# A gated mixture of experts after a conditional layer: hidden units numbered by chunk, the shared expert moved three tiles ahead, and the opening reordered

## The chip, the cores and the metric

The kernel runs on one core of one Trainium2 chip. The engines used are TensorE (PE), VectorE (DVE), ScalarE (ACT), GpSimd (POOL), and SyncE, whose queue (SPq) issues most of the DMAs. The metric is the device time of one execution in microseconds (us), lower is better.

## The reference, cut to what matters

```python
x = x + gelu(x @ W.T + fc_bias + z + cond)      # z: low-rank product with fside, per sample
# 32 samples of 128 tokens, 128 features; then a mixture of 4 experts and a shared one:
gate_logits = gate_in @ gate_w + gate_b         # gate_in: means over three token segments
gate_logits = gate_logits * (1.0 + scale) + shift
w_be = top-2 of softmax(gate_logits), renormalized
for e in range(4):                              # experts 1 and 2 skip one token segment
    h = gelu_tanh(x @ ew1[e] + eb1[e])          # 128 -> 512
    out += w_be[:, e] * mask[e] * (h @ ew2[e] + eb2[e])   # 512 -> 128
shared = gelu_tanh(x @ sw1 + sb1) @ sw2 + sb2
return x + out + shared
```

## The kernel before, in words

Features lie on the partitions, tokens on the free axis. The 32 samples make 8 tiles of 4 samples (512 tokens). The first four tiles pass the conditional layer at the start: transposes of x and fside, `matrices` (a 128x128 matrix per sample), `matrix` on DVE (adds W), `layer0`, `gelu0` on ACT, `residual` on DVE. Then each tile's x is split into a high and a low fp32r part (`x1_high` on ACT, `x1_low` on DVE), as are all expert weights (`weight_high` on ACT, `weight_low` on DVE), since each product is made as three fp32r matmuls (L449, L450, L451). Tiles 4 to 7 pass the conditional layer later, a step at a time between the experts (`late_tile`).

The middle layer has 512 hidden units in 4 chunks of 128. The work from there is a list `STEPS` of 40 units (t, s): tile t, s = 0 for the shared expert and 1 to 4 for the experts. Unit k goes through four stages:

- `up(k)` on PE: 4 chunks of 3 matmuls, each chunk into a PSUM bank of its own out of the ring `RING` (5 banks).
- `gelu(k)` on ACT: reads each bank, writes `h`. For a shared unit a second pass over the same bank writes `hs_hi`, the rounded high part; since `hs_hi` has two buffers, all of `gelu` for a shared unit waits until `down(k-2)` is done.
- `split(k)` on DVE: for an expert `hs_hi` (L695) and `hs_lo` (L700), both scaled by the sample's gate weight; for a shared unit `hs_lo` alone (L689).
- `down(k)` on PE: 12 matmuls that sum into `psY[t % 2]`, one bank per tile in work. When a tile's last unit is done, DVE adds it to x (`out_sum`), PE transposes, ACT copies out.

PE's order is written out by hand: `up(k + 2)`, then `down(k)`. A shared unit (t + 2, 0) stands behind the last expert of tile t; its `down` waits until `out_sum(t)` has read the sum bank of tile t. Experts 2 and 3 skip one segment and have 344 columns, the others 512. The gate of tiles 0 to 3 (`segment_sums`, `time_gate`, `gate_in`, `modulation`, `gate_logits`, `gate_weights` on DVE, two small products on PE, `gate_tanh` on ACT) runs at the start, and must be done before the first expert's `split`. POOL adds the output biases to x (L308) once they are known (`bias2_ok`).

The wait in `up` on the ring, and the one in `gelu`:

```python
                    else:
                        pe.wait_ge(h_ok, n - UP + 1)
...
                if s == 0 and k >= 2:
                    act.wait_ge(down_ok, k - 1)
```

Of the kernel before, what the change touches and what calls it, by code (L numbers as in the profile page):

```python
# [12 lines left out]
def build(nc, x, fside, cond, W, fc_bias, gate_w, gate_b, time_w, time_b,  # L13
# [40 lines left out]
    with ExitStack() as ctx:  # L54
# [18 lines left out]
        eb2_raw = sb("eb2_raw", [E, D])  # L73
        b1_col = sb("b1_col", [128, NS, CH])
# [80 lines left out]
            sem("tanh_g_ok"), sem("w_ok"), sem("bias2_ok"), sem("x1b_ok"))  # L155
        up_ps, h_ok, hi_ok, lo_ok, down_ok = sem("up_ps"), sem("h_ok"), sem("hi_ok"), sem("lo_ok"), sem("down_ok")
# [73 lines left out]
        def _(sp):  # L230
# [12 lines left out]
            def load_weight(n):  # L243
# [33 lines left out]
        def _(pool):  # L277
# [35 lines left out]
        def _(act):  # L313
# [49 lines left out]
            def gelu(k):  # L363
# [7 lines left out]
                for c in range(CH):  # L371
# [3 lines left out]
                    if s == 0:  # L375
# [71 lines left out]
        def _(pe):  # L447
# [5 lines left out]
            def keep_busy(n):  # L453
# [451 lines left out]
```

## Time and profile before

| | us |
|---|---|
| median of 3 runs | 276.78 (276.58 to 278.21) |
| the profiled execution | 276.94 |
| its span, first to last instruction | 274.8 |
| PE busy | 244.4 (89%) |
| DVE busy | 198.8 (72%) |
| ACT busy | 156.2 (57%) |
| POOL busy | 22.2 (8%) |

The span is 2.1 us shorter than the profiled execution's own time. A matmul's end is modelled in the profile and overlaps the next one, so the distance between two starts is what a matmul costs PE.

### The profile page before, as it was taken

To read this page: it belongs to the slowest core of one execution; us is meant where nothing else is said; L and a number is where in the kernel's file an instruction comes from. 1 tells how busy PE (TensorE), PEld (TensorE's weight loads), DVE (VectorE), ACT (ScalarE), POOL (GpSimd) and SP (SyncE) were. 2 spreads that over 40 slices of the span, in tenths; PEclk is the share of its full clock that TensorE was granted. 3 is DMA by queue.
4 is the path that set the end of the run, shared out by engine and by line. 5 is a ranking of instruction groups with operands and counts; after the bars stand their busy time and mean duration, and the time that the engine had idled before them with its cause. 6 is when DMAs were issued, how large, how long until landed. Compare 5 with 4: busy or idle time off the path is not lost.

```text
span 274.8 us, 3451 instructions
## 1 busy us (share of the span) xinstructions
PE 244.4 (89%) x1217; PEld 203.2 (74%) x1217; DVE 198.8 (72%) x441; ACT 156.2 (57%) x286; POOL 22.2 (8%) x39
## 2 busy tenths in 40 slices
PE   8964969799979997999989997999979989999963
PEld 7763748678768875888768885887768959898852
DVE  0266799999369565797399795797499959779661
ACT  4375799630894439760894439751835194544400
POOL 5000000940000000000000060000000600000000
PEclk9995598999999999999999999999999999999987
DMA  6995000000001000010001000010001000100101
GB/s 129 235 284 96 1 1 0 0 2 0 0 2 38 0 0 4 6 32 2 1 0 38 2 0 0 6 36 0 0 0 41 0 0 0 43 0 0 38 0 38
DMA packets 15811, 7.40 MB, mean 27 GB/s; under 512 B 6175, under 2 KB 14515, under 8 KB 15795
## 3 DMA queue, kind: packets, MB, share of 16 engines
q1 hardware_dynamic: 14781, 6.98, 10.6%
q10 hardware_dynamic: 854, 0.18, 0.3%
q8 instruction: 9, 0.15, 0.2%
q0 software_dynamic: 160, 0.02, 0.1%
q14 instruction: 7, 0.06, 0.1%
HBM read 5.09 MB, written 2.10 MB: 26 GB/s over the span
## 4 chain that ended last, share of the span: by engine, by line
PE 61%; ACT 16%; DVE 14%; issue 4%; DMA 2%; SPq 2%; DVEq 0%; ACTq 0%
PE ps L449 19%; PE ps L451 17%; PE ps L450 17%; ACT h L373 5%; ACT hs_hi L376 4%; DVE hs_lo L700 4%; DVE hs_hi L695 3%; PE ps L496 2%; DMA x_tok<-in_x 2%; DVE W_lo L679 2%; ACT L373 2%; ACT L354 2%; PE ps L508 2%; DVE hs_lo L689 2%; ACT W_raw L359 2%
## 5 line engine op out<-in xcount | busy, mean ns | idle before, releaser
L373 ACT ACTIVATE h<-ps,b_col 128x512 f32<-128x512 f32 (+1 forms) x160 | 94.1, 649 | 60.5 <-PE ps L451 38.4
L700 DVE SCALAR_TENSOR_TENSOR hs_lo<-h,w_be,hs_hi 128x512 fp32r<-128x512 f32 (+1 forms) x128 | 78.4, 673 | 0.0
L449 PE MATMUL ps<-x_hi,W_hi 128*128 128x512 f32 (+1 forms) x160 | 65.1, 407 | 14.2 <-ACT h L373 5.5
L449 PE MATMUL ps<-hs_hi,W_hi 128*128 128x512 f32 (+1 forms) x160 | 59.9, 375 | 6.3 <-DVE hs_lo L700 4.9
L695 DVE TENSOR_SCALAR hs_hi<-h,w_be 128x512 fp32r<-128x512 f32 (+1 forms) x128 | 50.3, 455 | 13.7 <-ACT h L373 6.9
L451 PE MATMUL ps<-x_lo,W_hi 128*128 128x512 f32 (+1 forms) x160 | 60.0, 375 | 0.0
L450 PE MATMUL ps<-x_hi,W_lo 128*128 128x512 f32 (+1 forms) x160 | 59.8, 374 | 0.0
L451 PE MATMUL ps<-hs_lo,W_hi 128*128 128x512 f32 (+1 forms) x160 | 59.0, 369 | 0.0
L450 PE MATMUL ps<-hs_hi,W_lo 128*128 128x512 f32 (+1 forms) x160 | 59.0, 369 | 0.0
L449 PEld LDWEIGHTS ps<-x_hi,W_hi 128*128 128x128 f32 x160 | 30.8, 192 | 27.9 <-ACT hs_hi L376 10.8
L449 PEld LDWEIGHTS ps<-hs_hi,W_hi 128*128 128x128 f32 x160 | 30.6, 191 | 11.6 <-DVE hs_lo L700 2.8
L689 DVE TENSOR_TENSOR hs_lo<-h,hs_hi 128x1024 fp32r<-128x1024 f32 x16 | 18.9, 1221 | 24.8 <-ACT hs_hi L376 24.8
L451 PEld LDWEIGHTS ps<-x_lo,W_hi 128*128 128x128 f32 x160 | 30.9, 193 | 4.5
L308 POOL TENSOR_TENSOR x<-x,bias 128x168 f32<-128x168 f32 (+1 forms) x24 | 18.2, 789 | 196.6 <-DVE bias L812 196.6
L451 PEld LDWEIGHTS ps<-hs_lo,W_hi 128*128 128x128 f32 x160 | 30.6, 191 | 4.3
L450 PEld LDWEIGHTS ps<-hs_hi,W_lo 128*128 128x128 f32 x160 | 30.7, 192 | 4.2
L450 PEld LDWEIGHTS ps<-x_hi,W_lo 128*128 128x128 f32 x160 | 31.1, 194 | 3.1
L376 ACT ACTIVATE hs_hi<-ps,b_col 128x512 fp32r<-128x512 f32 x32 | 22.8, 711 | 0.0
L391 ACT ACTIVATE x_tok<-ps 128x512 f32<-128x512 f32 x8 | 4.8, 598 | 28.6 <-PE ps L562 28.6
L327 ACT ACTIVATE x<-ps 128x512 f32<-128x512 f32 x8 | 4.8, 597 | 17.9 <-PE ps L466 17.9
L712 DVE TENSOR_TENSOR outT<-ps,x 128x168 f32<-128x168 f32 (+1 forms) x24 | 6.5, 327 | 5.3 <-PE ps L451 5.2
L654 DVE SCALAR_TENSOR_TENSOR h<-ps,WT 128x512 f32<-128x512 f32 x4 | 2.8, 689 | 9.3 <-PE ps L496 9.3
(102 smaller groups left out, 173.4 us busy)
## 6 DMA issues: line engine op xcount, KB each, us to landing
W_raw<-in_L_cond_ew SPq DMA_DIRECT2D x8, 256.0 KB, 4.9
out<-x_tok SPq DMA_DIRECT2D x8, 256.0 KB, 2.3
x_tok<-in_x SPq DMA_DIRECT2D x6, 168.0 KB
x_tok<-in_x SPq DMA_DIRECT2D x3, 176.0 KB
W_raw<-in_L_cond_sw SPq DMA_DIRECT2D x2, 256.0 KB, 5.0
x_tok<-in_x SPq DMA_DIRECT2D x3, 84.0 KB
F_raw<-in_fside_Bx1x1024x SPq DMA_DIRECT2D x3, 64.0 KB, 5.3
x_tok<-in_x SPq DMA_DIRECT2D x2, 88.0 KB
```

The source lines that it names most:

```text
L308: nc.gpsimd.tensor_tensor(xb[:, :, at:at + n], xb[:, :, at:at + n], bias2[:, i, t * NB:(t + 1) * NB].unsqueeze(2).to_broadcast([128, NB, n ...
L354: nc.scalar.activation(table_probe[:, 1:2], table_probe[:, 0:1], ACT.Gelu)
L359: ins = nc.scalar.activation(g0_late[:, b * L:(b + 1) * L], psLate[:, b * L:(b + 1) * L], ACT.Gelu, bias=bias0[:, t * NB + b:t * NB + b + 1])
L373: ins = nc.scalar.activation(span(h[:, k % 3, c, :], s), up_bank(k, c), ACT.Gelu_apprx_tanh, bias=b1_col[:, s, c:c + 1])
L376: ins = nc.scalar.activation(hs_hi[:, k % 2, c, :], up_bank(k, c), ACT.Gelu_apprx_tanh, bias=b1_col[:, s, c:c + 1])
L449: nc.tensor.matmul(dst, w_hi, m_hi, start=start, stop=False)
L450: nc.tensor.matmul(dst, w_lo, m_hi, start=False, stop=False)
L451: return nc.tensor.matmul(dst, w_hi, m_lo, start=False, stop=stop)
L689: nc.vector.tensor_tensor(hs_lo[:, k % 2, c:c + 2, :], h[:, k % 3, c:c + 2, :], f32(hs_hi[:, k % 2, c:c + 2, :]), ALU.subtract).then_inc(l ...
L695: nc.vector.tensor_scalar(hs_hi[:, k % 2, :, c], h[:, k % 3, :, c], w_be[:, t * NB + b, s - 1:s], None, ALU.mult).then_inc(hi_ok, 1)
L700: nc.vector.scalar_tensor_tensor(hs_lo[:, k % 2, :, c], h[:, k % 3, :, c], w_be[:, t * NB + b, s - 1:s], f32(hs_hi[:, k % 2, :, c]), ALU.m ...
L712: nc.vector.tensor_tensor(dst_v[:, :, dst:dst + n], sum_v[:, :, at:at + n], x1_v[:, :, at:at + n], ALU.add).then_inc(outT_ok, 1)
```

## The change

- The hidden units are numbered by chunk: unit c*128+p instead of 4p+c. The columns of the first weights that a chunk takes are then contiguous in SBUF instead of 16 bytes apart; the second weights come as four rows of 512 bytes for each partition instead of one of 2048. The biases `b1` come as 20 rows and are turned by a PE transpose and a DVE copy.
- `STEPS` begins with three shared units, and the shared unit behind tile t's last expert is that of tile t + 3. Bank 3 goes from the ring (now 4 banks) to `psY` (now 3).
- For a shared unit ACT writes the high part of two chunks only; DVE writes the other two with one cast from `h` (128x1024).
- In the opening DVE's `segment_sums`, `time_gate` and `output_rows` stand later; PE makes `up(0)` ahead of the gate's first product and `up(1)` ahead of its second, with six small products on ones in front; ACT rounds one more weight ahead of `gelu(0)`; `output_biases(0)` stands at unit 5.
- POOL waits, for tile t, until the split two units ahead of the tile's first expert is done.

```diff
-    STEPS = [(0, 0), (1, 0)]
+    AHEAD = 3
+    STEPS = [(t, 0) for t in range(AHEAD)]
     for t in range(NT):
         STEPS += [(t, s) for s in range(1, NS)]
-        if t + 2 < NT:
-            STEPS.append((t + 2, 0))
+        if t + AHEAD < NT:
+            STEPS.append((t + AHEAD, 0))
...
-    RING = [0, 1, 4, 2, 3]
+    RING = [0, 1, 4, 2]
...
-        psY = [ps[:, 5, :], ps[:, 6, :]]
+        psY = [ps[:, 5, :], ps[:, 6, :], ps[:, 3, :]]
...
-                return W1_raw[:, e, :].rearrange("p (m c) -> p c m", c=CH), W1_hi[:, e, :, :], W1_lo[:, e, :, :]
+                return W1_raw[:, e, :].rearrange("p (c m) -> p c m", c=CH), W1_hi[:, e, :, :], W1_lo[:, e, :, :]
...
-                    sp.dma_start(W2_raw[:, e, :], src.rearrange("(p c) d -> p (c d)", c=CH)).then_inc(w_in[n], 16)
+                    sp.dma_start(W2_raw[:, e, :].rearrange("p (c d) -> p c d", c=CH),
+                                 src.rearrange("(c p) d -> p c d", c=CH)).then_inc(w_in[n], 16)
...
+                pool.wait_ge(lo_ok, parts_until(first_step(t) - 2))
...
-                    if s == 0:
+                    if s == 0 and c < CH // 2:
                         ins = nc.scalar.activation(hs_hi[:, k % 2, c, :], up_bank(k, c), ACT.Gelu_apprx_tanh,
...
-                if s == 0 and t >= 2:
-                    pe.wait_ge(outT_ok, NSEG * (t - 1))
+                if s == 0 and t >= AHEAD:
+                    pe.wait_ge(outT_ok, NSEG * (t - AHEAD + 1))
...
                 if s == 0:
+                    nc.vector.tensor_copy(hs_hi[:, k % 2, CH // 2:, :], h[:, k % 3, CH // 2:, :]).then_inc(shared_hi_ok, 1)
                     for c in range(0, CH, 2):
+                        if c == CH // 2:
+                            dve.wait_ge(shared_hi_ok, t + 1)
```

DVE's order in the opening, before, from the residual of tile 1 on (h<-ps,WT is `matrix`, segsum `segment_sums`, the rows from silu2 to gw `time_gate`):

```order
L661 TENSOR_TENSOR x1<-x1,h 128x512
L666 TENSOR_TENSOR x1_lo<-x1,x1_hi 128x512
L673 TENSOR_REDUCE segsum<-x1 128x8 x3
L717 SCALAR_TENSOR_TENSOR silu2<-tanh_c,condT 128x32
L720 TENSOR_SCALAR tw<-time_w_raw 128x8
L722 TENSOR_TENSOR mod_terms<-silu2,tw 128x256
L726 TENSOR_SCALAR gw_full<-gate_raw 128x4
L727 SCALAR_TENSOR_TENSOR gw<-gate_raw,gw_full 128x4
L729 SCALAR_TENSOR_TENSOR gw<-gate_raw,gw_full 128x4
L730 SCALAR_TENSOR_TENSOR gw<-gate_raw,gw 128x4
L736 COPY eb2T<-ps 128x4 x3
```

The `matrix` of tile 3 stands behind all of these. The same place on DVE now:

```order
L674 TENSOR_TENSOR x1<-x1,h 128x512
L679 TENSOR_TENSOR x1_lo<-x1,x1_hi 128x512
L667 SCALAR_TENSOR_TENSOR h<-ps,WT 128x512
L674 TENSOR_TENSOR x1<-x1,h 128x512
L679 TENSOR_TENSOR x1_lo<-x1,x1_hi 128x512
L753 COPY eb2T<-ps 128x4 x3
L755 COPY b1_col<-ps 128x20
L757 MEMSET eb2T 128x1
L758 MEMSET eb2T 128x1
L692 TENSOR_TENSOR W1_lo<-W1_raw,W1_hi 128x512
L686 TENSOR_REDUCE segsum<-x1 128x8 x3
```

The `matrix` of tile 3 now comes right behind the low part of tile 0, and the low part of the first weight ahead of all gate work.

ACT's order at a shared unit that is followed by a late tile's gelu, before (it repeats for every late tile):

```order
L373 ACTIVATE h<-ps,b1_col 128x512 x5
L376 ACTIVATE hs_hi<-ps,b1_col 128x512
L373 ACTIVATE h<-ps,b1_col 128x512
L376 ACTIVATE hs_hi<-ps,b1_col 128x512
L373 ACTIVATE h<-ps,b1_col 128x512
L376 ACTIVATE hs_hi<-ps,b1_col 128x512
L373 ACTIVATE h<-ps,b1_col 128x512
L376 ACTIVATE hs_hi<-ps,b1_col 128x512
L354 ACT_TABLE_LOAD
L354 ACTIVATE table_probe<-table_probe 128x1
L359 ACTIVATE W2_raw<-ps,bias0 128x128 x4
L373 ACT_TABLE_LOAD
```

And now:

```order
L381 ACTIVATE h<-ps,b1_col 128x512 x5
L384 ACTIVATE hs_hi<-ps,b1_col 128x512
L381 ACTIVATE h<-ps,b1_col 128x512
L384 ACTIVATE hs_hi<-ps,b1_col 128x512
L381 ACTIVATE h<-ps,b1_col 128x512 x2
L362 ACT_TABLE_LOAD
L362 ACTIVATE table_probe<-table_probe 128x1
L367 ACTIVATE W2_raw<-ps,bias0 128x128 x4
L381 ACT_TABLE_LOAD
```

Two of the eight passes over the unit's banks are gone from ACT.

## Rows read from the trace of the kernel before

**Rows 1.** The page, part 2: granted TensorE clock in tenths, 40 slices of 6.87 us

```profile
PEclk9995598999999999999999999999999999999987
```

**Rows 2.** View of the waits, whole run: us in total, times, longest

```profile
PE ps L449 <- ACT h L373: 5.5, 4, 1.5
...
PE ps L449 <- DVE W_lo L679: 4.9, 2, 2.7
...
PE ps L449 <- ACT hs_hi L376: 3.8, 14, 0.7
```

**Rows 3.** Timeline of the opening: start, length, engine, line; idle before and releaser

```profile
18.73 1.33 DVE L673 TENSOR_REDUCE segsum<-x 128x8 f32<-128x336 f32 x3
...
21.74 0.69 DVE L654 SCALAR_TENSOR_TENSOR h<-ps,WT 128x512 f32<-128x512 f32 x1
...
22.54 2.05 PE L508 MATMUL ps<-x,h 128*128 128x128 f32 x8 [3.99 <-issue]
...
24.62 1.14 ACT L348 ACTIVATE h<-ps,bias 128x128 f32<-128x128 f32 x4 [3.39 <-PE ps L508]
...
28.12 0.80 PE L449 MATMUL ps<-x_hi,W_hi 128*128 128x512 f32 x1 [2.68 <-DVE W_lo L679]
...
29.85 1.28 ACT L373 ACT_TABLE_LOAD   x1 [1.54 <-PE ps L451]
...
33.77 0.23 DVE L766 TENSOR_TENSOR logit<-ps,gate_mul 128x64 f32<-128x64 f32 x1 [1.69 <-PE ps L576]
...
37.08 1.68 DVE L679 TENSOR_TENSOR W_lo<-W_raw,W_hi 128x512 fp32r<-128x512 f32 x2
```

**Rows 4.** Stretches of 1 us: busy by engine, granted clock, DMA share, GB/s

```profile
15.00:16.00 1.00, 1.00 (x11) 0.96 (x10) 0.81 (x2) 0.99 (x2) 0.00 (x0) 1.00 1.06 397
...
20.00:21.00 1.00, 0.00 (x0) 0.00 (x0) 0.91 (x6) 1.00 (x2) 0.00 (x0) 0.50 1.05 154
```

**Rows 5.** Timeline of the first units (35 to 70 us)

```profile
48.62 9.69 POOL L308 TENSOR_TENSOR x<-x,bias 128x168 f32<-128x168 f32 x12 [43.45 <-DVE bias L812]
...
51.84 3.60 DVE L700 SCALAR_TENSOR_TENSOR hs_lo<-h,w_be,hs_hi 128x512 fp32r<-128x512 f32 x4
...
55.59 0.47 PE L449 MATMUL ps<-hs_hi,W_hi 128*128 128x512 f32 x1 [2.37 <-DVE hs_lo L700]
```

**Rows 6.** Timeline around one shared unit in the middle (70 to 90 us)

```profile
69.81 0.69 ACT L373 ACTIVATE h<-ps,b_col 128x512 f32<-128x512 f32 x1 [7.28 <-PE ps L451]
...
74.24 0.39 PE L449 MATMUL ps<-hs_hi,W_hi 128*128 128x512 f32 x1
...
74.56 1.28 ACT L354 ACT_TABLE_LOAD   x1
...
76.99 0.32 PE L449 MATMUL ps<-x_hi,W_hi 128*128 128x344 f32 x1
...
78.40 4.17 ACT L373 ACTIVATE h<-ps,b_col 128x512 f32<-128x512 f32 x8
79.14 0.43 PE L449 MATMUL ps<-x_hi,W_hi 128*128 128x344 f32 x1 [1.51 <-ACT h L373]
...
80.85 1.67 DVE L695 TENSOR_SCALAR hs_hi<-h,w_be 128x512 fp32r<-128x512 f32 x4 [2.31 <-ACT h L373]
80.88 0.40 PE L449 MATMUL ps<-hs_hi,W_hi 128*128 128x512 f32 x1
...
85.09 1.32 DVE L695 TENSOR_SCALAR hs_hi<-h,w_be 128x344 fp32r<-128x344 f32 x4
```

**Rows 7.** View by tile, `W_hi` and `W_lo`: length in ns, min/median/max

```profile
L323 ACT ACTIVATE W_hi<-W_raw x10: 641/942/1280, 20.1 to 49.1; 128x512 fp32r<-128x512 f32 x10
L679 DVE TENSOR_TENSOR W_lo<-W_raw,W_hi x10: 679/1005/1253, 27.0 to 61.6; 128x512 fp32r<-128x512 f32 x10
```

**Rows 8.** Timeline at the last gate group (190 to 204 us)

```profile
192.46 0.50 PE L449 MATMUL ps<-x_hi,W_hi 128*128 128x512 f32 x1 [0.71 <-ACT hs_hi L376]
...
202.03 0.50 PE L449 MATMUL ps<-hs_hi,W_hi 128*128 128x512 f32 x1 [1.40 <-DVE outT L712]
```

More of the change, by code:

```diff
@@ L415, in _ @@
             weight_high(WEIGHTS[2])
-            act.wait_ge(b1_in, 32)
+            weight_high(WEIGHTS[3])
+            act.wait_ge(b1_ok, 1)
             gelu(0)
             gate_tanh(0)
-            weight_high(WEIGHTS[3])
             gelu(1)
@@ L451, in product3, with keep_busy @@
                 return nc.tensor.matmul(dst, w_hi, m_lo, start=False, stop=stop)
-            def keep_busy(n):
+            def keep_busy(n, dst=psIdle):
                 for _ in range(n):
-                    nc.tensor.matmul(psIdle, ones[:, :], ones[:, :], start=True, stop=True)
+                    nc.tensor.matmul(dst, ones[:, :], ones[:, :], start=True, stop=True)
             def xT(t):
@@ L539, in down @@
                     pe.wait_ge(w_lo_ok, made(2 * s + 1))
-                if s == 0 and t >= 2:
-                    pe.wait_ge(outT_ok, NSEG * (t - 1))
+                if s == 0 and t >= AHEAD:
+                    pe.wait_ge(outT_ok, NSEG * (t - AHEAD + 1))
+                elif s == 0 and t == 2:
+                    pe.wait_ge(g0_ok, NA)
                 elif s == 0 and t == 1:
@@ L546, in down @@
                 for c in range(CH):
[L547 removed]
+                    last = product3(span(psY[t % AHEAD], s), W2_hi[:, s, c, :], W2_lo[:, s, c, :],
                                     span(hs_hi[:, k % 2, c, :], s), span(hs_lo[:, k % 2, c, :], s),
@@ L601, in _ @@
                     nc.tensor.transpose(psEb2T, eb2_raw[:, :], ident[0:E, 0:E]).then_inc(eb2T_ps, 1)
+                    pe.wait_ge(b1_in, 16 * 2)
+                    nc.tensor.transpose(psB1, b1_rows[:, :], ident[0:NS * CH, 0:NS * CH]).then_inc(b1_ps, 1)
+            keep_busy(6, ps[:, 6, 0:128])
+            up(0)
             pe.wait_ge(eb2T_read, NSEG)
+            pe.wait_ge(b1_ok, 1)
             pe.wait_ge(mod_terms_ok, 1)
             nc.tensor.matmul(psMod, ones[:, :], mod_terms[:, :, :], start=True, stop=True).then_inc(mod_ps, 1)
-            up(0)
+            up(1)
             logits(0)
-            up(1)
             for k in range(K):
@@ L709, in out_sum @@
                 dst_v, sum_v, x1_v = (ap.rearrange("p (b l) -> p b l", l=L)
-                                      for ap in (outT[:, t % 2, :], psY[t % 2], x1[:, t, :]))
+                                      for ap in (outT[:, t % 2, :], psY[t % AHEAD], x1[:, t, :]))
                 for at, dst, n in SEGS:
@@ L827, in _ @@
                     x1_low(t - 1)
-                if t == 1:
+                if t == 2:
+                    output_rows()
+                    weight_low(WEIGHTS[0])
                     segment_sums(0, 2)
-                    time_gate()
-                    output_rows()
-            weight_low(WEIGHTS[0])
             segment_sums(2, 4)
+            time_gate()
             gate_in(0)
+            x1_low(NA - 1)
             dve.wait_ge(bias_in, 16 * 3)
             modulation()
-            x1_low(NA - 1)
-            gate_logits(0)
             weight_low(WEIGHTS[1])
             weight_low(WEIGHTS[2])
+            gate_logits(0)
             split(0)
@@ L844, in _ @@
             split(1)
-            weight_low(WEIGHTS[4])
-            output_biases(0)
-            weight_low(WEIGHTS[5])
+            for n in WEIGHTS[4:6]:
+                weight_low(n)
             for k in range(2, K):
```

15 lines of the change are left out of this document (10 added, 5 removed).

## The prediction, made before the changed kernel ran

> **What bounds the kernel now.** I read the page's clock line, then the waits of PE, then the timeline at each place where PE waits. PE sets the end: it is 89% busy, and its work is the same in both kernels but for a few small products, so only its waiting and its clock can change. A chunk of three 512-column matmuls costs 0.69 us: from 74.24 to 76.99 twelve of them run without a gap, 0.23 us each [rows 6]. PE's lost time lies in four places.
> (a) The opening. DVE works on the segment sums at 18.73 and gets to tile 3's `matrix` only at 21.74; `layer0` of tile 3 starts at 22.54, after 3.99 us idle, and by 20 us the granted clock is at 0.50, its lower level [rows 3, 4]. `up(0)` starts at 28.12, held by the first weight's low part, and its matmuls run at that level [rows 1, 3].
> (b) The first units. PE waits 2.2 us for a low weight (4.9 in two waits, 2.7 of it at 28.12) and 2.37 for `hs_lo` of the first expert, which ends late since POOL's twelve adds run beside it: that `hs_lo` takes 3.60 us, while a whole split of 512 columns elsewhere takes 4.24, from 80.85 to 85.09 [rows 2, 3, 5, 6].
> (c) Each shared unit in the middle. ACT may start it only when `down(k-2)` is done, then makes eight passes at 0.58 us (69.81 to 74.56), and behind them, at four of the six, a late tile's gelu with two table loads. PE waits on its banks (14 waits of 3.8 us in all) and then 1.5 us for the next gelu [rows 2, 6].
> (d) Near 202 us: `down` of a shared unit waits 1.40 us for `out_sum`, which stands behind the gate's work on DVE [rows 8].
>
> **The opening, step by step.** Until 18.7 nothing moves by more than 0.2 us (one 20-row transpose more; the bias rows are issued earlier than before). Tile 3's `matrix` takes DVE's place of 18.73 and ends at 19.4, `layer0` follows until 20.4 (full clock) or 21.3 (half). DVE then has residual and low part of tile 1 and 2 (0.6 us each), the small copies, and the first `weight_low`: 22.4. ACT's first `weight_high` is of the contiguous kind, 0.64 us instead of 1.12, and `weight_low` 0.68 instead of 1.06: the two ends of Rows 7, since the second weights were contiguous before and the first were not [rows 7]. The six small products fill PE until 21.7 to 23.5. So `up(0)` starts at 22.5 to 23.5 instead of 28.12, at full clock for 2.76 us: done by 25.2 to 26.3.
> ACT: `gelu0` of tile 3 (1.14 us) ends at 22.2, then high parts; it waits for DVE's residual of tile 3 (24.35, behind 1.33 us of segment sums), rounds two more weights (26.3), loads the table (1.28) and makes six passes: chunks are free at 28.8, 29.9, 30.5 and 31.1. Before, the load began at 29.85 [rows 3]: 3.6 us later. `up(1)` follows these chunks and ends at 32.0, or at 33.5 if the clock has fallen during PE's waits; the gate's product follows, and DVE's `gate_logits` starts at 32.3 to 33.8, where it was at 33.77 [rows 3]. Here almost all of the opening's gain is given back: the gate chain is as late as before. It takes 3.3 us as before (33.77 until the two weights at 37.08 [rows 3]). Then `split(0)`: two subtractions as before and a cast, 2.3 + 0.7 us.
> The cast has one source and 1024 columns. Below: the same rate as the one-source L695, which takes 1.67 us for four of 512 and 1.32 us for four of 344, so 0.52 ns per column, 0.42 + 512 x 0.00052 = 0.68 us. Above: the two-source rate, twice the 0.68 of a contiguous `weight_low`, 1.36 us [rows 6, 7]. I take 0.7, the nearer kind of instruction. Of what no row shows, the Trainium skill, "VectorE: DVE Perf Modes", section "Mode 2×_2P — use both read ports for one tensor", says that a one-source copy within SBUF makes two results a cycle even in fp32 and a two-source one can't; by it the cast would be near the lower bound, by the other bound DVE has 0.7 us more in each of eight units.
> So `split(0)` ends at 38.6 to 40.1, `down(0)` (2.75 us) at 41.3 to 42.8. Now a new wait: the third unit, (2,0), is a shared one, so `gelu(2)` starts only at the end of `down(0)`, D. Its chunks are free at D + 1.2, 2.3, 2.9, 3.5; `up(3)` ends at D + 4.2 (1.4 us lost), `down(1)` at D + 7.0, `up(4)` at D + 8.9, `down(2)` at D + 11.7, `up(5)` and the late transposes at D + 14.1. DVE ends `split(2)` at D + 7.4 and the first expert's at D + 12.9 (4.3 us, without POOL beside it), so PE no longer waits there. Then `down(3)`, the first expert's, begins at 55.4 to 56.9, where it was at 55.59 [rows 5], but with one more shared unit done, 24 x 0.23 = 5.5 us of PE work. A last 0.4 us comes from the order of the late tile's work. **Gain of the opening:** 5.5 + 0.4 + (55.59 - 55.4) = 6.1, or 4.6 at the late end; with 1.2 us more off if the clock falls a second time between `up(1)` and `up(2)`, 3.4. I take 4.9.
>
> **A shared unit in the middle.** With four banks a chunk of the next `up` waits for the same chunk's gelu, not for the chunk before. In Rows 6's case chunks are free at 71.1, 72.2, 72.8, 73.4 (two with two passes, two with one); the fourth chunk runs 73.7 to 74.4, and `down` starts at 74.4 instead of 74.24: the ring costs what the two passes save. Behind it ACT's last pass ends at 73.4 instead of 74.56, so table loads, late gelu and the next gelu are 1.15 us early: that gelu starts at 77.25 instead of 78.40 and its four chunks, 0.58 us apart, are free at 77.9, 78.5, 79.1, 79.7. The following `up` (344 columns, 0.48 us a chunk) ends at 80.2 instead of 80.88 [rows 6]: gain 0.68. Four such units: **2.7**. DVE's cast is hidden: DVE was idle 2.31 us ahead of 80.85 [rows 6]; were it not, it would cost 0.7 a unit.
> There are now five shared units in the middle instead of six, and the one that goes is without a late gelu; PE lost 0.71 us in one wait there [rows 8], 0.2 in each of the two that follow it and about 0.5 in slowed starts: **1.6**. The one in the opening is counted above.
>
> **The third sum bank.** `down` of a shared unit waits for a sum of three tiles back, long read. The 1.40 us goes, with 0.2 of slowed start [rows 8]; next late is `hs_lo` of the following expert, 1.8 us away from PE's new arrival minus the cast. **1.6.**
>
> **The rest at nothing.** The second weights come in short rows. While long rows land the DMAs move 397 GB/s, while x's 512-byte rows land 154 [rows 4]: 256 KB take 1.7 us instead of 0.66, five loads some 5 us more. The last would land near 24 us and is rounded after 48; cover gone only if the first, wanted at 22.9, came 8 us late. POOL's adds now run in threes beside DVE's idle time ahead of a shared unit; if not, 2.4 us of POOL stretch DVE by 0.9 us x 3/12 each. The tail (PE waits for the last `hs_lo`, and the clock falls behind it [rows 1]) is unchanged.
>
> **Sum.** 4.9 + 2.7 + 1.6 + 1.6 = 10.8 off the profiled 276.94 gives 266.1, off the median 266.0.
>
> **Rivals.**
> 1. The ring takes the middle's gain. If a short ring costs a chunk (0.69) at each of five shared units instead of 0.15, 2.7 us go, and another 0.8 where no late gelu follows: 266.0 + 3.5 = 269.5. For it: PE already waits on the banks 14 times. Against: the start times above. Chance 0.17.
> 2. The clock stays low through the opening. PE's work from 25 to 40 us is now in pieces with waits of 1 to 2.5 us, and in this trace the clock fell in a wait of 3.99 us and again after the one of 2.2 (the seventh slice) [rows 1, 3]. At half clock a chunk costs 1.28 instead of 0.69: `up(1)`, `up(2)`, `down(0)` and `up(3)` 16 x 0.59 = 9.4, of which waits cover nearly half; 4.9 us are lost: 270.9. Chance 0.10. The Trainium skill, "TensorE: Matmul & The Clock Gate", section "What's actually happening", has the same thing as a rule: the throttled state is the default and activity releases it; by it the six filling products are too few for these waits.
> 3. Slower: four banks bind at every unit. `up(k+2)` can't start until `gelu(k+1)` has freed its first bank; that is hidden as long as ACT is less than one `down` (1.9 to 2.75 us) behind. If ACT fell behind by more, each of 37 units would lose a chunk's gelu less the cover, 0.35 us or more: 13 us, so 279. It decides from ACT's lag of 2.75 us on. Against: ACT is 57% busy, and away from shared units PE has no wait on it [rows 2]. Chance 0.04.
> 4. The opening gives nothing: DVE, busy without a pause, gets the casts and a third split ahead of the first expert and is late by as much as PE gains. 266.0 + 4.9 = 270.9, and with rival 1 274.4, no change. 0.05 for the first, 0.04 for the second.
>
> **Chances.** The forecast (264 to 268.5) 0.60; rivals 0.17, 0.10, 0.04, 0.09. The range must take in rivals 1 and 2 and, below, an opening at full clock with DVE's last waits gone (2 us): 263.0 to 271.5. A difference under 1% is about what a measurement of this kernel can't tell. Faster by over 1% (below 274.0) 0.90, within 1% 0.06, slower 0.04.
>
> **What would show it.** In the new trace: `up(0)` starts near 23 at the clock's upper level; `gate_logits` near 33; the first expert's `down` near 56, without a wait; PE's wait behind each late gelu about 0.8 instead of 1.5; no wait of PE on `outT`; the cast 0.7 us. Wrong if PE waits on `h` at ordinary units, if the cast takes 1.2 us or more, or if the clock line shows more fives than before.

## The result, and the profile after

| | before | after |
|---|---|---|
| median, us (range, runs) | 277.24 (276.58 to 278.21, 4) | 268.47 (265.95 to 271.4, 4) |
| the profiled execution | 276.94 | 265.95 |
| its span | 274.8 | 264.2 |
| mean granted clock in it | 0.958 | 0.996 |
| PE busy | 244.4 (89%) | 239.3 (91%) |
| DVE busy | 198.8 (72%) | 197.3 (75%) |
| ACT busy | 156.2 (57%) | 145.4 (55%) |
| POOL busy | 22.2 (8%) | 15.2 (6%) |

The ratio after to before is 0.959, with a 95% interval of 0.954 to 0.965; it and the ratios of the experiments leave out executions over 1.5% above the fastest of their kernel, and the two medians alone give 0.968. The median stands between two levels at which the changed kernel comes out, 265.95 and 266.08 us at a mean granted clock of 0.996 and 0.990, and 270.86 and 271.4 at 0.975 and 0.973; the profiled execution is one of the upper clock.

The page's clock line, that answers to [rows 1]:

```profile
PEclk9999999999999999999999999999999999999998
```

No slice is below nine tenths but the last: the two fives and the eight of the opening are gone. The view of the waits of PE (in all, times, longest), that answers to [rows 2]:

```profile
PE ps L457 <- ACT hs_hi L384: 8.5, 12, 2.6
PE ps L457 <- DVE hs_lo L717: 2.5, 1, 2.5
PE ps L457 <- ACT h L381: 2.2, 4, 0.6
PE ps L457 <- DVE outT L729: 1.9, 2, 1.4
...
PE ps L457 <- DVE hs_lo L706: 0.4, 1, 0.4
PE ps L457 <- DVE W_lo L692: 0.3, 1, 0.3
```

The wait for low weights went from 4.9 to 0.3 us and that for the late gelu (`h`) from 5.5 to 2.2. The wait on the banks (`hs_hi`) grew from 3.8 to 8.5, 2.6 of it once in the opening, and `outT` is still there. The opening's timeline (start, length, engine, line; idle before and releaser), answering to [rows 3, 5]:

```profile
19.07 1.13 PE L516 MATMUL ps<-x,h 128*128 128x128 f32 x8 [0.90 <-issue]
...
21.80 0.50 PE L457 MATMUL ps<-x_hi,W_hi 128*128 128x512 f32 x1 [0.26 <-DVE W_lo L692]
...
28.02 0.47 PE L457 MATMUL ps<-x_hi,W_hi 128*128 128x512 f32 x1 [1.12 <-DVE x_lo L679]
...
31.63 0.23 DVE L785 TENSOR_TENSOR logit<-ps,gate_mul 128x64 f32<-128x64 f32 x1 [1.04 <-PE ps L584]
...
34.22 0.47 PE L457 MATMUL ps<-x_hi,W_hi 128*128 128x512 f32 x1 [2.62 <-ACT hs_hi L384]
...
38.04 0.47 PE L457 MATMUL ps<-hs_hi,W_hi 128*128 128x512 f32 x1 [0.40 <-DVE hs_lo L706]
...
42.57 0.47 PE L457 MATMUL ps<-x_hi,W_hi 128*128 128x512 f32 x1 [1.50 <-ACT hs_hi L384]
```

`layer0` of tile 3 waits 0.90 us instead of 3.99, and `up(0)`, `up(1)`, `up(2)`, `down(0)` and `up(3)` start at 21.80, 28.02, 34.22, 38.04 and 42.57. The middle shared unit of [rows 6]:

```profile
69.78 0.69 ACT L381 ACTIVATE h<-ps,b_col 128x512 f32<-128x512 f32 x1 [7.28 <-DVE hs_lo L717]
...
71.11 0.50 PE L457 MATMUL ps<-x_hi,W_hi 128*128 128x512 f32 x1 [0.52 <-ACT hs_hi L384]
...
73.40 0.69 DVE L702 CAST hs_hi<-h 128x1024 fp32r<-128x1024 f32 x1 [3.63 <-ACT h L381]
...
74.47 0.40 PE L457 MATMUL ps<-hs_hi,W_hi 128*128 128x512 f32 x1
...
77.23 4.18 ACT L381 ACTIVATE h<-ps,b_col 128x512 f32<-128x512 f32 x8
...
77.97 0.43 PE L457 MATMUL ps<-x_hi,W_hi 128*128 128x344 f32 x1 [0.58 <-ACT h L381]
```

The late gelu's successor starts at 77.23, 1.17 us earlier than in [rows 6], and PE waits 0.58 us for it instead of 1.51. The place of [rows 8]:

```profile
200.43 0.50 PE L457 MATMUL ps<-hs_hi,W_hi 128*128 128x512 f32 x1 [1.40 <-DVE outT L729]
```

The length of this wait is unchanged: the one that the third sum bank was thought to remove is still 1.40 us.

### The profile page after: what moved, and what is told of

The parts are those of the page before. It is cut to its first block, busy times and chain, and to the rows that moved or that the text cites. A ratio compares the mean times of both kernels' runs of the same rounds, so it can differ in the third digit from the quotient of the medians.

```text
span 264.2 us, 3479 instructions
## 1 busy us (share of the span) xinstructions
PE 239.3 (91%) x1230; PEld 200.3 (76%) x1230; DVE 197.3 (75%) x450; ACT 145.4 (55%) x270; POOL 15.2 (6%) x39
## 3 DMA queue, kind: packets, MB, share of 16 engines
q1 hardware_dynamic: 16069, 6.98, 10.8%
## 4 chain that ended last, share of the span: by engine, by line
PE 69%; ACT 14%; DVE 11%; issue 4%; DVEq 0%; POOL 0%; ACTq 0%; POOLq 0%
PE ps L457 20%; PE ps L459 19%; PE ps L458 19%; ACT h L381 5%; DVE hs_lo L717 4%; PE ps L504 3%; ACT hs_hi L384 3%; DVE hs_hi L712 3%; ACT L381 2%; PE ps L474 2%; PE ps L463 2%; PE ps L488 1%; ACT L362 1%; PE ps L570 1%; ACT W_raw L367 1%
## 5 line engine op out<-in xcount | busy, mean ns | idle before, releaser
L381 ACT ACTIVATE h<-ps,b_col 128x512 f32<-128x512 f32 (+1 forms) x160 | 92.7, 641 | 63.8 <-PE ps L459 38.0
L717 DVE SCALAR_TENSOR_TENSOR hs_lo<-h,w_be,hs_hi 128x512 fp32r<-128x512 f32 (+1 forms) x128 | 76.2, 657 | 0.0
L457 PE MATMUL ps<-x_hi,W_hi 128*128 128x512 f32 (+1 forms) x160 | 63.3, 395 | 12.5 <-ACT hs_hi L384 8.5
L459 PE MATMUL ps<-x_lo,W_hi 128*128 128x512 f32 (+1 forms) x160 | 58.5, 366 | 0.0
L458 PE MATMUL ps<-x_hi,W_lo 128*128 128x512 f32 (+1 forms) x160 | 58.5, 365 | 0.0
L712 DVE TENSOR_SCALAR hs_hi<-h,w_be 128x512 fp32r<-128x512 f32 (+1 forms) x128 | 48.5, 441 | 12.2 <-PE ps L459 7.9
L458 PEld LDWEIGHTS ps<-x_hi,W_lo 128*128 128x128 f32 x160 | 30.2, 189 | 3.1
L316 POOL TENSOR_TENSOR x<-x,bias 128x168 f32<-128x168 f32 (+1 forms) x24 | 11.1, 491 | 215.9 <-DVE hs_lo L717 134.1
L702 DVE CAST hs_hi<-h 128x1024 fp32r<-128x1024 f32 x8 | 5.5, 692 | 17.4 <-ACT h L381 17.4
L384 ACT ACTIVATE hs_hi<-ps,b_col 128x512 fp32r<-128x512 f32 x16 | 11.0, 689 | 0.0
```

Source lines behind the costliest of these rows:

```text
L316: nc.gpsimd.tensor_tensor(xb[:, :, at:at + n], xb[:, :, at:at + n], bias2[:, i, t * NB:(t + 1) * NB].unsqueeze(2).to_broadcast([128, NB, n ...
L381: ins = nc.scalar.activation(span(h[:, k % 3, c, :], s), up_bank(k, c), ACT.Gelu_apprx_tanh, bias=b1_col[:, s, c:c + 1])
L384: ins = nc.scalar.activation(hs_hi[:, k % 2, c, :], up_bank(k, c), ACT.Gelu_apprx_tanh, bias=b1_col[:, s, c:c + 1])
L457: nc.tensor.matmul(dst, w_hi, m_hi, start=start, stop=False)
L458: nc.tensor.matmul(dst, w_lo, m_hi, start=False, stop=False)
L459: return nc.tensor.matmul(dst, w_hi, m_lo, start=False, stop=stop)
```

## The experiments

All start from the changed kernel; the medians of before on the same chips were 277.1, 277.5 and 277.3 us. The table has medians in us with range and number of executions, the ratio to before with its 95% interval, and the mean granted clock of each execution. Differences of medians below hold the clock too; where two kernels stand at different levels, the text also compares executions at like clocks, or the starts of the same `down` in the two profiles.

| run | median (range, runs) | ratio [95%] | clocks |
|---|---|---|---|
| act_writes_all | 275.6 (273.1 to 279.5, 10) | 0.995 [0.990, 1.000] | .963 to .996 |
| old_dve_opening | 273.0 (271.9 to 273.5, 4) | 0.984 [0.980, 0.988] | .962 .966 .962 .962 |
| old_numbers | 272.7 (268.9 to 273.2, 4) | 0.976 [0.966, 0.985] | .972 .962 .977 .966 |
| two_ahead | 264.5 (263.2 to 265.3, 4) | 0.957 [0.951, 0.962] | .989 .985 .990 .983 |
| two_ahead_ring4 | 269.2 (268.8 to 270.0, 4) | 0.974 [0.970, 0.979] | .978 .978 .976 .990 |
| sum_before_gate | 269.2 (265.7 to 269.7, 4) | 0.966 [0.958, 0.975] | .990 .968 .968 .968 |
| fill_waits | 266.0 (265.6 to 267.3, 5) | 0.958 [0.954, 0.962] | .994 .994 .994 .994 .996 |
| no_six | 268.3 (265.4 to 270.8, 4) | 0.960 [0.953, 0.967] | .975 .982 .971 .990 |
| pool_free | 269.3 (265.8 to 271.8, 4) | 0.962 [0.955, 0.970] | .989 .990 .968 .967 |
| dve_casts_all | 256.4 (255.3 to 258.2, 4) | 0.928 [0.922, 0.935] | .975 .980 .980 .980 |
| best_two_ahead | 254.8 (254.7 to 258.2, 4) | 0.924 [0.916, 0.931] | .995 .982 .999 .989 |
| best_sum_first | 252.5 (252.2 to 252.6, 4) | 0.912 [0.907, 0.917] | .996 to .999 |

**The cast undone: act_writes_all.** ACT writes the high part of all four chunks again, nothing else is changed.

```diff
-                    if s == 0 and c < CH // 2:
+                    if s == 0:
...
-                    nc.vector.tensor_copy(hs_hi[:, k % 2, CH // 2:, :], h[:, k % 3, CH // 2:, :]).then_inc(shared_hi_ok, 1)
...
-                        if c == CH // 2:
-                            dve.wait_ge(shared_hi_ok, t + 1)
```

> The changed kernel with ACT writing the high part of all four chunks of a shared unit, and no cast on DVE. Theory A (ACT's passes are on the path at every shared unit): each of five middle units ends 0.85 to 1.15 us later, the opening 1 to 2: 271 to 273 us. Rival (the passes are hidden, the change's gain comes from the opening alone): 266 to 267.

Measured: 7 us slower than the change, more than expected, and the same between the two executions at a clock of .996 (273.1 against 265.95); what is left can't be told from before. The first line of the view of PE's waits:

```profile
PE ps L457 <- ACT hs_hi L384: 11.2, 26, 2.6
```

The banks now hold PE 26 times instead of 12, and the starts of ACT at the shared units lie 31.4 us apart (72.22, 103.59, 134.94) instead of 30.2. With a ring of four banks the two passes that the cast saves are worth 1.15 us for each middle unit.

**The opening on DVE undone: old_dve_opening.** `segment_sums(0, 2)`, `time_gate` and `output_rows` stand behind the residual of tile 1 again.

```diff
+                dve.wait_ge(b1_ps, 1)
...
+                if t == 1:
+                    segment_sums(0, 2)
+                    time_gate()
+                    output_rows()
                 if t == 2:
-                    output_rows()
                     weight_low(WEIGHTS[0])
-                    segment_sums(0, 2)
             segment_sums(2, 4)
-            time_gate()
```

> The changed kernel with DVE's segment sums, time gate and small rows back ahead of tile 3's matrix. Theory A (tile 3 comes 3 us later, the clock falls in that wait, and gelu(0) starts 3 us later): 3 to 5 us more than the changed kernel. Rival (DVE does the same work in either order and is the bound of the opening): within 1 us.

Measured: 4.6 us slower at the medians, clock included; in the profiles the first expert's `down` starts at 59.62 instead of 55.55. PE again waits for tile 3's `matrix`, `up(0)` starts at 25.82 instead of 21.80, and the clock falls in every execution (.962 to .966). One line of the view of PE's waits, and the clock line of this kernel:

```profile
PE ps L516 <- issue: 3.9, 1, 3.9
```

```profile
PEclk9986979899999999999999999999979999999979
```

**The numbering undone: old_numbers.** Weights, their loads and the biases are laid out as before (unit 4p+c).

```diff
-                return W1_raw[:, e, :].rearrange("p (c m) -> p c m", c=CH), W1_hi[:, e, :, :], W1_lo[:, e, :, :]
+                return W1_raw[:, e, :].rearrange("p (m c) -> p c m", c=CH), W1_hi[:, e, :, :], W1_lo[:, e, :, :]
...
-                    sp.dma_start(W2_raw[:, e, :].rearrange("p (c d) -> p c d", c=CH),
-                                 src.rearrange("(c p) d -> p c d", c=CH)).then_inc(w_in[n], 16)
+                    sp.dma_start(W2_raw[:, e, :], src.rearrange("(p c) d -> p (c d)", c=CH)).then_inc(w_in[n], 16)
```

> The changed kernel with the hidden units numbered as before (columns 16 bytes apart, long rows of the second weights, biases loaded in place). Theory A (three first weights stand on ACT ahead of the first gelu, 0.5 us each, and one on DVE ahead of up(0), 0.4): the opening is 1.5 to 2.5 us later, and the clock falls more often: 2 to 5 us more than the changed kernel's median of 268.5. Rival (hidden): within 1 us.

Measured: 4.2 us slower at the medians, 2.9 between the fastest executions, which is what was expected. `up(0)` starts at 22.60 and the first gelu at 28.38 instead of 26.61, behind weights that ACT rounds at the slow rate of [rows 7]; the clock is lower too (.962 to .977).

**Two tiles ahead: two_ahead and two_ahead_ring4.** The first has `AHEAD` 2, the ring of five (and the wait for its fifth bank's first use) and two sum banks, as before, with all else of the change; the second is the same without the line of `RING`.

```diff
-    AHEAD = 3
+    AHEAD = 2
...
-    RING = [0, 1, 4, 2]
+    RING = [0, 1, 4, 2, 3]
...
-        psY = [ps[:, 5, :], ps[:, 6, :], ps[:, 3, :]]
+        psY = [ps[:, 5, :], ps[:, 6, :]]
```

> The changed kernel with the shared expert two tiles ahead again, so with five ring banks and two sum banks; everything else of the change stays. Theory A (the gain is the opening's order, plus one middle shared unit fewer): the opening loses nothing, one shared unit more stands in the middle and costs 1.6 us; 267 to 268 us against 266 in executions at the upper clock. Rival (three ahead is what hides the gate at the start): the first expert's split comes too late for PE, 3 us or more are lost, 270 or above.

> As two_ahead, but with four ring banks, bank 3 unused: the price of the fifth bank alone. Theory A (a chunk waits for ACT's pace either way, 0.15 us per middle shared unit): within 0.8 us of two_ahead. Rival (the ring binds at shared units, 0.7 us at each of six): 4 us more than two_ahead.

Measured: 264.5 and 269.2. The first is faster than either of its expectations. The fifth bank is worth 4.7 us at the medians and 4.3 between the executions at a clock of .990 (264.54 and 268.85). Of the change's parts the step to three tiles ahead, bought with that bank, costs 1.5 us against the change's executions at the upper clock (266.0), and 4.0 at the median, where the change's lower level counts too. The step alone, with four banks in both kernels, gains: 268.85 against 266.08 at .990, 2.8 us. PE's largest waits, of two_ahead and then of two_ahead_ring4:

```profile
PE ps L457 <- ACT hs_hi L384: 4.9, 11, 1.8
PE ps L457 <- ACT h L381: 3.0, 4, 0.8
PE ps L457 <- DVE hs_lo L719: 2.5, 1, 2.5
PE ps L457 <- DVE outT L731: 1.8, 2, 1.4
```

```profile
PE ps L457 <- ACT hs_hi L384: 8.6, 13, 2.6
...
PE ps L457 <- ACT h L381: 2.2, 4, 0.6
PE ps L457 <- DVE outT L729: 1.9, 2, 1.4
```

With five banks the wait on the ring is 3.7 us less and that for `h` 0.8 more; the shared units follow each other at 29.6 us (63.17, 92.80, 122.43) and not at 30.2 (66.17, 96.38, 126.61). In the profiles 3.0 of the two kernels' difference is there by the first expert's `down` (48.95 and 51.97), and 3.8 come after it. These are the timelines of `up(1)`, with five banks and with four:

```profile
28.02 0.50 PE L457 MATMUL ps<-x_hi,W_hi 128*128 128x512 f32 x1 [0.34 <-ACT hs_hi L384]
```

```profile
28.26 0.77 PE L457 MATMUL ps<-x_hi,W_hi 128*128 128x512 f32 x1 [1.12 <-DVE x_lo L679]
```

At 28.02 the first is in its second chunk, having made one from 26.64 on in the free bank; the second only begins, and at half clock (0.77 us for the matmul), so a part of the 3.0 is clock. And `outT` is waited for with two banks and two ahead just as with three and three.

**The late gate behind the sum: sum_before_gate.** `gate_logits` of a late group moves from ahead of `out_sum` to behind it.

```diff
                 if s == NS - 1:
                     out_sum(t)
+                g = late_gate(k, 5)
+                if g is not None:
+                    gate_logits(g)
                 split(k)
...
-                g = late_gate(k, 4)
-                if g is not None:
-                    gate_logits(g)
```

> The changed kernel with gate_logits of the late groups behind out_sum on DVE instead of ahead of it. Theory A (a shared unit's down still waits for the sum of the tile just finished, since t + 3 and t have the same of three banks): PE's waits for outT, 1.4 and 0.5 us, go: 1.5 to 2 us less than the changed kernel. Rival (PE then waits for hs_lo of the next expert, as gate_logits delays that all the same): under 0.5 us.

Measured: 265.67 in one execution, 268.7 to 269.7 at a clock of .968 in three. Of the change's executions two took 265.95 and 266.08, and two took 270.9 and 271.4. The time of the profiled execution, 0.3 us less than the change's, hides what the edit does; the two profiles show it. First the last `down` of the changed kernel, then of this one:

```profile
256.29 0.50 PE L457 MATMUL ps<-hs_hi,W_hi 128*128 128x512 f32 x1 [2.54 <-DVE hs_lo L717]
```

```profile
203.62 0.51 PE L457 MATMUL ps<-hs_hi,W_hi 128*128 128x512 f32 x1 [0.36 <-DVE hs_lo L717]
...
254.43 0.50 PE L457 MATMUL ps<-hs_hi,W_hi 128*128 128x512 f32 x1 [2.54 <-DVE hs_lo L717]
```

Both waits on the sum bank are gone. `down(7,0)` starts at 197.96 instead of 200.43, the `down` behind it waits 0.36 us for `hs_lo`, and the last `down` starts 1.9 us earlier: 0.8 of that comes from the wait at 141 us and 1.0 from that at 200 us. Then the clock takes 1.6 us of it back. The stretch, columns as in [rows 4]:

```profile
256.00:257.00 1.00, 1.00 (x4) 0.71 (x3) 0.00 (x0) 0.00 (x0) 0.00 (x0) 0.50 0.00 0
```

The last `down` takes 4.60 us here and 3.04 in the changed kernel's profile. So theory A holds, and not the rival.

**The clock: fill_waits and no_six.** The first puts small products on ones, whose sums nobody reads, into PE's waits: 6 behind `up(0)`, 2 ahead of `up(1)`, 11 behind the gate's product, 10 ahead of the last `down`. The second leaves out the six that the change has ahead of `up(0)`.

```diff
             up(0)
+            keep_busy(6, ps[:, 6, 0:128])
...
+            keep_busy(2, ps[:, 6, 0:128])
             up(1)
             logits(0)
+            keep_busy(11, ps[:, 6, 0:128])
...
+                if k == K - 1:
+                    keep_busy(10, ps[:, 3, 0:128])
```

> The changed kernel with small products on ones in PE's waits of the opening (6 behind up(0), 2 ahead of up(1), 11 behind the gate's product) and 10 ahead of the last down; nothing waits for them. Theory A (the change's executions at 271 us are those in which the granted clock falls in the opening's waits): no execution above 267, median 265 to 266.5, mean clock 0.99 or more in each. Rival (the spread has another cause): the executions at 271 stay.

> The changed kernel without the six small products ahead of up(0). Theory A (they hide nothing and only keep PE active through a wait of 1.7 us): at the upper clock the same 266 us, but up(0) or up(1) run at the lower clock more often: median 269 to 272. Rival (the clock there hangs on the real work alone): no change from 268.5, within 0.5.

Measured: with the fillers five executions at .994 to .996 and none at 271; the best time is not lower than without them (265.6 against 265.95), so they take away the lower level and no more. Of the change, no_six, pool_free and sum_before_gate together, 7 executions of 16 are at the upper level, so five of five is unlikely to be chance. The fillers do not cover the wait ahead of `up(3)`, and in the profiled execution, the slowest of the five (267.26), the clock falls behind it (1.49 us at 42.50) and `down(1)` starts 1.5 us later than in the changed kernel's profile:

```profile
45.00:46.00 1.00, 1.00 (x3) 0.74 (x3) 1.00 (x3) 1.00 (x3) 0.00 (x0) 0.50 0.00 0
```

Without the six nothing moves (268.3 against 268.5, both levels again). The profiled execution of no_six happens to be one of the lower level, and its stretches show where those executions lose (columns as in [rows 4]; first the same stretch of the changed kernel's profile, then three of no_six):

```profile
36.00:37.00 1.00, 1.00 (x6) 0.80 (x5) 1.00 (x2) 1.00 (x3) 0.00 (x0) 1.00 0.00 0
```

```profile
36.00:37.00 1.00, 1.00 (x3) 0.72 (x3) 1.00 (x2) 1.00 (x3) 0.00 (x0) 0.50 0.00 0
...
196.00:197.00 1.00, 1.00 (x4) 0.81 (x3) 1.00 (x2) 0.69 (x1) 0.00 (x0) 0.50 0.00 0
...
261.00:262.00 1.00, 1.00 (x4) 0.80 (x3) 0.00 (x0) 0.00 (x0) 0.00 (x0) 0.50 0.00 0
```

Behind the wait of 2.6 us ahead of `up(2)`, and again at 45 to 48 us, the granted clock is 0.50 (1.2 GHz), and PE has 3 or 4 matmuls in a microsecond instead of 6. `down(1)` starts at 47.84 and the first expert's `down` at 57.60, 2.0 us after the changed kernel's 45.83 and 55.55. The other 2.8 of the 4.9 us between the two profiles are not in the opening. 1.5 go at 194 to 198 us, behind a wait of 1.41 us that the changed kernel's profile has as well (at 190.60) and keeps its full clock behind, and 1.3 in the last `down`.

**POOL's new wait left out: pool_free.**

```diff
-                pool.wait_ge(lo_ok, parts_until(first_step(t) - 2))
```

> The changed kernel without POOL's wait for the split, so that nine adds for tiles 1 to 3 follow those of tile 0 at once, beside DVE's split of the fourth expert. Theory A (PE's slack behind that split is 4.7 us): no change, within 0.5 us of the changed kernel at the same clock. Rival (the adds stretch DVE into PE's path): 1 to 2 us more.

Measured: 265.8 and 267.0 in its two executions at the upper clock, the change 265.95 and 266.08; POOL is busy for 19.4 us instead of 15.2. The wait moves the adds to DVE's idle time, and the last `down` starts at 256.10 without it, 256.29 with it.

**All high parts on DVE: dve_casts_all.** ACT makes four passes in a shared unit and no longer waits for `down(k-2)`; DVE makes two casts of 1024 columns.

```diff
-                if s == 0 and k >= 2:
-                    act.wait_ge(down_ok, k - 1)
...
-                    if s == 0 and c < CH // 2:
-                        ins = nc.scalar.activation(hs_hi[:, k % 2, c, :], up_bank(k, c), ACT.Gelu_apprx_tanh,
-                                                   bias=b1_col[:, s, c:c + 1])
...
-                    nc.vector.tensor_copy(hs_hi[:, k % 2, CH // 2:, :], h[:, k % 3, CH // 2:, :]).then_inc(shared_hi_ok, 1)
...
+                        nc.vector.tensor_copy(hs_hi[:, k % 2, c:c + 2, :], h[:, k % 3, c:c + 2, :]
+                                              ).then_inc(shared_hi_ok, 1)
+                    for c in range(0, CH, 2):
+                        dve.wait_ge(shared_hi_ok, 2 * t + c // 2 + 1)
```

> The changed kernel with ACT writing no high part: DVE casts all four chunks, and so ACT's gelu of a shared unit no longer waits for the down two units back. Theory A (that wait, not the passes' number, makes PE wait at shared units): PE's 1.2 to 2 us at each of five middle units and 1.5 us in the opening go, DVE has 0.7 us more per unit, which it does in idle time: 258 to 261 us. Rival (DVE becomes the bound at the unit behind a shared one): 264 to 266.

Measured: 12 us faster than the change at the medians, more than expected. Against the change's two executions at the upper clock it is 9.6, and this kernel's own clock is lower; in the profiles the last `down` starts at 246.15 instead of 256.29, 10.1 us earlier. The view of PE's waits, and the timeline of the same shared unit:

```profile
PE ps L452 <- DVE outT L725: 2.8, 2, 1.4
PE ps L452 <- ACT h L379: 2.6, 2, 2.0
PE ps L452 <- DVE hs_lo L713: 2.5, 1, 2.5
```

```profile
66.38 2.72 ACT L379 ACTIVATE h<-ps,b_col 128x512 f32<-128x512 f32 x4 [3.30 <-PE ps L454]
...
70.40 1.57 DVE L698 CAST hs_hi<-h 128x1024 fp32r<-128x1024 f32 x2
...
70.42 3.30 POOL L316 TENSOR_TENSOR x<-x,bias 128x168 f32<-128x168 f32 x3 [4.29 <-DVE hs_lo L713]
71.89 2.91 DVE L702 TENSOR_TENSOR hs_lo<-h,hs_hi 128x1024 fp32r<-128x1024 f32 x2
```

No wait on `hs_hi` is left, and the shared units start 27.8 us apart (66.38, 94.17) instead of 30.2. ACT's pause ahead of the unit is 3.30 us where the changed kernel's is 7.28 (the row of 69.78), 4.0 us less, while the two passes saved are worth 1.2 (0.58 us each, as in [rows 6]). So most of it can be put down to the wait for `down(k-2)`, which ACT had because it wrote into a buffer that `down` reads. That is argued from the pauses: the edit takes away the passes and the wait together, and the passes without the wait were not tried. DVE's `split` waited for the same `down` before and still does. The clock is still .975 to .980.

**Put together: best_two_ahead and best_sum_first.** The first is two_ahead with dve_casts_all and fillers (6 behind `up(0)`, 6 inside `up(2)`, 11 and 6 behind `up(2)` and `up(3)`, 10 ahead of the last `down`); the second adds the edit of sum_before_gate.

> Shared expert two tiles ahead with five ring banks and two sum banks, all casts of shared units on DVE, small products on ones in PE's waits of the opening and ahead of the last down; the rest as in the changed kernel. Theory A (the gains of two_ahead, 4 us, of dve_casts_all, 12 us, and of fill_waits, 2 us, are at different places): 250 to 254 us, little spread. Rival (with ACT out of the way DVE is the bound and the ring no longer matters): 255 to 257, as dve_casts_all.

> As best_two_ahead, with out_sum ahead of the late groups' gate_logits on DVE. Theory A (DVE is busy without a pause there, so the wait moves from outT to hs_lo): within 0.7 us of best_two_ahead. Rival: 1.5 us less.

Measured: 254.8, between its two expectations, and 252.5, and the second is the fastest kernel of the study: 16.0 us below the change's median, 13.5 below its executions at the upper clock. Its page and its view of waits:

```profile
PE 242.4 (97%) x1308; PEld 210.4 (84%) x1308; DVE 204.3 (81%) x458; ACT 139.2 (56%) x254; POOL 29.7 (12%) x39
```

```profile
PE ps L452 <- DVE W_lo L696: 1.0, 2, 0.8
PE ps L569 <- DVE outT L734: 0.9, 1, 0.9
...
PE ps L452 <- DVE hs_lo L722: 0.6, 2, 0.3
```

(The `outT` of L569 is the transpose at the very end, not the sum bank.) The move of `gate_logits` gives 2.3 us at the medians and 2.2 at the start of the last `down` (242.79 against 244.97), by the same mechanism as in sum_before_gate: best_two_ahead has two waits of 1.40 us on the sum bank, and in best_sum_first they are gone and 0.3 us is waited for `hs_lo` in their place. best_two_ahead's own gain over dve_casts_all is 1.2 us at the start of the last `down` (244.97 against 246.15), 1.6 at the medians. So the fifth bank, worth over 4 us while ACT made PE wait on the banks, is worth about 1 once it doesn't, fillers included. With 39 fillers one execution of best_two_ahead still came out at 258.2 and .982.

## Why the prediction was right, and where it was not

**The time.** 266.1 was forecast for the profiled execution, and it took 265.95. The median of 268.5 lies in the range, 2.5 us above the 266.0. The median is above because half of the executions are at the lower clock. That the sum was met to 0.2 us is in part luck: under it stand one term that was wrong, one that was too large, and two gains that made up for them.

**The opening, 4.9.** Right, and slightly low. The first steps are 0.2 to 0.7 us ahead of their ranges: `up(0)` starts at 21.80 (22.5 to 23.5 forecast), `gate_logits` at 31.63 (32.3 to 33.8), `down(0)` ends at 41.1 (41.3 to 42.8), and the first expert's `down` at 55.55 (55.4 to 56.9), without a wait. The matching later unit, the third expert of tile 0, ends at 69.70 where it ended at 69.72, with the 5.5 us of a third shared unit done besides: 5.5 gained. As forecast, most of what `up(0)` wins is given back: 6.3 us at `up(0)`, 2.1 at the gate. old_dve_opening and old_numbers show both halves of the term: either undone costs 4 us or more, clock included.

**The cast, 0.7.** Measured 0.69 us (mean 692 ns over eight), the lower bound. At the middle units it is hidden, since DVE had idled 2.5 to 4.0 us ahead of it; in the opening it stands in DVE's unbroken work ahead of `down(0)`, which waits 0.40 us for `hs_lo`, and the forecast counted it there. The rule of the Trainium skill that was cited there ("VectorE: DVE Perf Modes", section "Mode 2×_2P — use both read ports for one tensor") agrees: at the same width the two-source `hs_lo` takes 1.22 us (mean of sixteen).

**A middle shared unit, 0.68 each, 2.7 in all.** The timing of the unit in [rows 6] was met to 0.1 us: `down` at 74.47 (74.4), the gelu behind the late tile at 77.23 (77.25), PE at 77.97 (77.9), the second `down` at 80.28 (80.2). ACT's starts at 69.78, 100.01, 130.22, 161.21 and 189.28 stood at 69.81, 100.61, 131.41, 162.51 and 191.14 before: gains of 0.58, 0.59, 0.11 and 0.56 for the four units with a late gelu, together 1.8. The third has most of the shortfall, from the wait on `outT` of 0.48 us at 141.37, which was at nothing in the forecast. The size of the term was off, not its mechanism.

**One middle unit fewer, 1.6.** From 189.28 to the end it is 74.92 us, before (from 191.14) 83.66. That is 8.74 less, 5.5 of it the unit's own work, and so 3.2 gained. About 1.6 of that is the tail (next but one), which leaves about 1.7 for this term.

**The third sum bank, 1.6.** This step failed. The prediction said that "`down` of a shared unit waits for a sum of three tiles back, long read". But the unit that stands behind tile t is that of tile t + 3, and with three banks (t + 3) % 3 is t % 3: it wants the bank of the tile that has just ended, whose sum DVE has not read yet. The same holds of two ahead with two banks, so there was nothing that could change, and the wait stayed at 1.40 us; a second of 0.48 came up. The term is 0 where 1.6 was written. What it would have been worth had the wait gone, sum_before_gate shows: the 1.40 us and the new 0.48 away, the last `down` starts 1.9 us earlier, 1.0 of it by the wait of the forecast. The next wait, `hs_lo`, comes in as the forecast said that it would, but sooner than "1.8 us away", with 0.36 us. That four sum banks, or three with two tiles ahead, would remove the wait follows from the index; no run has them.

**The tail, at nothing.** In the profiled execution the clock stays at its upper level behind the last wait of 2.54 us, where before it fell to 0.50 behind the same wait: the last `down` takes 3.04 us instead of 4.60. First a stretch of the kernel before, then one of the changed kernel (columns as in [rows 4]):

```profile
266.00:267.00 1.00, 1.00 (x4) 0.81 (x3) 0.00 (x0) 0.00 (x0) 0.00 (x0) 0.50 0.00 0
```

```profile
257.00:258.00 1.00, 1.00 (x6) 0.81 (x5) 0.00 (x0) 0.00 (x0) 0.00 (x0) 1.00 0.00 0
```

That is some 1.6 us that no edit of the change explains, and it offsets the missing bank: luck of the execution, since sum_before_gate and no_six have the longer tail behind the same wait. So the profiled sum reads, measured: 5.5 + 1.8 + 1.7 + 0 + 1.6 = 10.6, which is the difference of the two spans. The forecast was 10.8, and 11.0 was found, 0.4 of it outside the span.

**Rival 2, the clock through the opening.** It was given 0.10 and a time of 270.9, and half of the executions come out at 270.86 and 271.4. The number is hit by luck: the change's own executions at that level have no profile, and in the one of no_six that has, the opening loses 2.0 us and not 4.9; 1.5 go at 194 to 198 us and 1.3 in the last `down`. Nor is it another way in which the kernel goes, but a second level that other executions of the same kernel do not have, and it is why the median is above the forecast. That PE's waits are the cause is borne out by fill_waits: with small products in the waits of the opening and in the last one, five executions of five are at .994 or more, and in its profile the one fall is behind a wait without them. The rule cited there from the Trainium skill, that activity releases the clock ("TensorE: Matmul & The Clock Gate", section "What's actually happening"), agrees in kind. So does what the prediction drew from it, that the six products ahead of `up(0)` are too few for these waits: without them the kernel is as fast. Why the clock falls behind a wait in one execution and not behind the same wait in another stays open.

**Rival 1, the ring.** Half true. A ring of four instead of five costs 0.58 us for each middle unit: the units lie 31.37 us apart in act_writes_all and 30.80 in the kernel before, 30.21 in two_ahead_ring4 and 29.63 in two_ahead. That is nearer to the rival's 0.69 than to the 0.15 of the forecast. But the two passes save 1.15, not what the ring costs, and so the middle's gain came after all. Against the comparison that matters for a choice, the fifth bank kept (two_ahead), the change loses 1.5 us at the upper clock.

Rivals 3 and 4 did not come: PE has no wait on `h` at ordinary units, and the opening gained what it should. Of what was to be hidden, POOL's wait costs nothing (pool_free), and the short rows of the second weights show no wait. Their price was far too high in the forecast: from 13 to 17 us, while the weights land, the DMAs move 308 to 343 GB/s in the changed kernel and 338 to 397 before, and in both the last traffic of the opening is at 24 to 25 us. The 154 GB/s of [rows 4] come from a stretch of 1 us in which not only rows of x but also rows of `fside`, 64 bytes each and issued at 17.81 us, can have been on their way.

## What to carry to other kernels

Before a deeper buffer is credited with removing a wait, write down the index that the waiting instruction takes and who used it last: a consumer that runs n ahead in a ring of n is back at the buffer just used, and by the index needs n + 1, which no run here has. An engine that writes into a double buffer takes over the reader's lateness; moving the rounding to the engine that has slack at that point was worth some 10 us here. And where PE must wait for microseconds in a one-core kernel, look at the clock of several executions, since one profile shows only one of them. A few products into an idle bank made the spread smaller, where they stood in the waits. To judge an edit worth 1 or 2 us, compare where the same late instruction starts in the two profiles: here the tail's clock hid 1.6 of the 1.9 us that the move of `gate_logits` gives.

## What the runs showed of the hardware

- The same program comes out at a mean granted clock of .990 to .996 or .973 to .975, 266 or 271 us. With 29 small products in the waits (58 more matmuls in the page, 1288 for 1230) it was .994 or more in five of five.
- Behind the same wait the granted clock falls in one execution and not in another: behind 1.41 us at 190.60 it stays at 1.00 in the changed kernel's profile, and in that of no_six (at 192.57) it is at 0.50 from 195 to 197 us. It also fell behind waits of 1.49 us (fill_waits, no_six) and 2.54 us (before, no_six, sum_before_gate), and stayed behind 2.62 and 2.54 us in the changed kernel's profile. At 0.50 the last `down` takes 4.60 us instead of 3.04.
- POOL's add of 128x168 takes 0.44 us where DVE is idle (three in 1.33 us), 0.81 us beside the late splits of an expert ([rows 5]) and 1.10 beside DVE's casts and `hs_lo` (three in 3.30). At 70, 98 and 126 us of dve_casts_all, where this is so, DVE is stretched too: two casts take 1.57 us instead of 1.29, and two of `hs_lo` 2.91 instead of 2.35. At 156.8 us three adds take 5.18 us beside the same work, and DVE's times are the undisturbed ones (1.28 and 2.35).
- Rounding a weight of 128x512 from contiguous columns takes 0.66 us on ACT and 0.69 on DVE (means of ten), where [rows 7] had 0.64 to 1.28 and 0.68 to 1.25.
